# Attention and feed-forward on one core: projections dealt between the halves of second-layer units, a warmed beginning, and a last norm in halves

## The reference, cut to what matters

```python
qkv = (x @ w_qkv.T + b_qkv).reshape(b, n, 3, H, D).transpose(2, 0, 3, 1, 4)
q, k, v = qkv[0], qkv[1], qkv[2]
q, k = elu(q) + 1.0, elu(k) + 1.0
q, k = _apply_rope(q, sin, cos), _apply_rope(k, sin, cos)
attn = softmax(einsum('bhnd,bhmd->bhnm', q, k) * scale)
attn_out = einsum('bhnm,bhmd->bhnd', attn, v)
lepe = conv1d(v over the tokens, w_lepe, 3 taps, one channel each) + b_lepe
x = layernorm(x + attn_out + lepe)
# feed-forward: _conn_dense(k, h) is h @ where(k, 1, -1)
h = concatenate([x, -x]); h = relu(s0 * _conn_dense(k0, h)) * 2    # first layer, 1024 wide
h = relu(s1 * _conn_dense(k1, h)) * 2                              # second layer, 1024 wide
x = layernorm(x + s2 * _conn_dense(k2, h))                         # third layer, 256 wide
```

## Time and profile before

| | |
|---|---|
| median of 3 runs | 2167.17 us (2163.6 to 2169.74) |
| the profiled execution's own time | 2168.84 us |
| its span from first to last instruction | 2166.8 us |
| PE busy | 2077.0 us, 96% |
| DVE busy | 1696.8 us, 78% |
| ACT busy | 1499.5 us, 69% |
| POOL busy | 1008.6 us, 47% |
| first exponential of step 0 | 89.24 us |
| first and second batch, from first exponential to first exponential | 198.8 us, 238.5 us |
| each of the third to seventh | 254.7 us |
| last exponential | 2053.6 us |

### The profile page before, as it was taken

One profiled execution on the slowest core, in us unless ns is written; L12 is line 12 of the kernel. 1 busy time (PEld: TensorE's weight loads), 2 busy tenths in 40 slices (PEclk: granted clock), 3 DMA queues, 4 the chain that ended last, 5 costly groups with the idle time before them and its releaser, 6 DMA issues.

```text
span 2166.8 us, 43669 instructions
## 1 busy us (share of the span) xinstructions
PE 2077.0 (96%) x17136; PEld 836.7 (39%) x17136; DVE 1696.8 (78%) x3094; ACT 1499.5 (69%) x2867; POOL 1008.6 (47%) x578
## 2 busy tenths in 40 slices
PE   4899999999999999999999999999999999999988
PEld 2123333344433434334343443434343343434345
DVE  7978998787887887878787887878878788877143
ACT  3299888766777667776777767776677766767532
POOL 2849269432866157472584427761475704300000
PEclk8689999999999999999999999999999999999999
DMA  5101200010010200111001200002001110000000
GB/s 179 33 9 37 82 19 26 26 67 21 16 34 20 89 16 9 35 58 49 16 25 26 83 25 17 28 16 96 11 17 36 31 57 16 16 9 28 1 1 39
DMA packets 40428, 76.87 MB, mean 35 GB/s; under 512 B 15024, under 2 KB 19488, under 8 KB 37280
## 3 DMA queue, kind: packets, MB, share of 16 engines
q1 hardware_dynamic: 35040, 51.02, 8.2%
q0 software_dynamic: 5184, 23.07, 2.8%
HBM read 46.27 MB, written 25.17 MB: 33 GB/s over the span
## 4 chain that ended last, share of the span: by engine, by line
PE 79%; DVE 13%; ACT 5%; issue 2%; DMA 0%; POOL 0%; SPq 0%; POOLq 0%; ACTq 0%; DVEq 0%
PE unit_banks L723 25%; PE unit_banks L587 21%; PE o_bank L632 19%; DVE maxima L987 8%; PE unit_banks L736 5%; PE unit_banks L659 4%; ACT probs L814 3%; PE unit_banks L597 2%; PE unit_banks L647 1%; DVE hT L1056 1%; DVE h0T L1059 1%; DVE stats L1133 1%; PE unit_banks L640 0%; ACT work L856 0%; ACT work L855 0%
## 5 line engine op out<-in xcount | busy, mean ns | idle before, releaser
L987 DVE TENSOR_REDUCE maxima<-unit_banks 128x1 f32<-128x512 f32 x2048 | 1307.4, 684 | 326.2 <-PE unit_banks L587 321.3
L814 ACT ACTIVATE probs<-unit_banks 128x512 f32<-128x512 f32 x2048 | 1118.7, 599 | 540.3 <-PE unit_banks L597 536.5
L587 PE MATMUL unit_banks<-k_stack,q_stack 48*128 48x512 f16 x2048 | 660.3, 392 | 26.0 <-DVE maxima L987 22.4
L597 PE MATMUL unit_banks<-q_stack,k_stack 50*128 50x512 f16 x2048 | 657.3, 387 | 6.3 <-ACT probs L814 4.2
L632 PE MATMUL o_bank<-probs,v_pair 128*32 128x256 f32 x8192 | 565.4, 388 | 0.5
L723 PE MATMUL unit_banks<-h0T,w 128*128 128x512 f16 x2048 | 480.1, 380 | 0.0
L1385 POOL TENSOR_TENSOR attn<-o_rows_sb,rden 128x256 f32<-128x256 f32 x63 | 39.2, 622 | 787.9 <-DVE rden L1000 774.3
L587 PEld LDWEIGHTS unit_banks<-k_stack,q_stack 48*128 48x128 f16 x2048 | 155.1, 94 | 525.9 <-DVE maxima L987 273.5
L632 PEld LDWEIGHTS o_bank<-probs,v_pair 128*32 128x32 f32 x8192 | 207.5, 109 | 297.0 <-issue 216.9
L723 PEld LDWEIGHTS unit_banks<-h0T,w 128*128 128x128 f16 x2048 | 189.4, 98 | 222.8 <-issue 33.1
L597 PEld LDWEIGHTS unit_banks<-q_stack,k_stack 50*128 50x128 f16 x2048 | 155.5, 93 | 46.3 <-ACT probs L814 37.0
(11 more groups left out here) (148 smaller groups left out, 1664.0 us busy)
## 6 DMA issues: line engine op xcount, KB each, us to landing
rows<-in_x POOLq DMA_DIRECT2D x8, 1024.0 KB, 5.9
q_stack<-q_scratch SPq DMA_DIRECT2D x128, 64.0 KB, 2.0
k_stack<-k_scratch SPq DMA_DIRECT2D x128, 64.0 KB, 2.0
work<-in_xT SPq DMA_DIRECT2D x7, 1024.0 KB, 6.9
q_scratch<-parts POOLq DMA_DIRECT2D x14, 512.0 KB, 3.3
k_scratch<-parts POOLq DMA_DIRECT2D x14, 512.0 KB, 3.2
out<-rows SPq DMA_DIRECT2D x7, 1024.0 KB, 4.9
q_stack<-q_scratch SPq DMA_DIRECT2D x128, 32.0 KB, 1.9
```

Of the source, the lines that this page charges most:

```text
L587: nc.tensor.matmul(units.out(unit), q_stack[row:row + STACK, r, t * P:(t + 1) * P], k_stack[row:row + STACK, r, half * 512:(half + 1) * 51 ...
L597: nc.tensor.matmul(units.out(unit), k_stack[row:end, r, kt * P:(kt + 1) * P], q_stack[row:end, r, half * 512:(half + 1) * 512], start=True ...
L814: nc.scalar.activation(probs[:, 2 * (kt % 2) + h, half * 512:(half + 1) * 512], units.out(unit), ACT.Exp, scale=exp_regs[2 * (n % PAIRS) + ...
L987: nc.vector.reduce_max(maxima[:, v // T % 2, h * T + t, half:half + 1], units.out(unit), AXIS_X)\
```

## The change

1. **Table of the dense work.** `proj` units stand on every second step, from step 6 for Q (6, 8, 10, 12 instead of 6 to 9) and from step 28 for K (28, 30, 32, 34 instead of 32 to 35); in the second batch's projections, which run in the first batch, K has 22, 24, 26, 28 instead of 22 to 25. Pieces of `L1` units fill the steps between (7, 9, 11, 13 and 29, 31, 33, 35). The scale units move by one and three steps. The four input maxima stand on steps 55, 57, 59, 61 instead of 55 to 58, and the `bound` unit on step 62 instead of 59.
2. **Beginning.** 14 transposes of `ident` into `o_bank` on PE ahead of everything; POOL's load of the first rows (`load_x(0)`) moves behind its set-up and the arrival of the row constants; the nine small constants move on DVE ahead of the first elu, and the subtraction that makes `w0` is cut into two, one ahead of each `low_start`; all V results come after K's low part; K's scratch stores are issued by ACT; the Q stacks are loaded before K is stored.
3. **End.** POOL adds seven of the eight pairs of columns to the last rows as soon as they are there, DVE only the last one; the sums of that norm, its scales and the late units are interleaved in halves; the sums of the norm before it come after the first `L1` unit of the tail.

```diff
 Q_AT = 6
-K_AT, SCALE_AT = {1: 22}, ({}, {1: 28})
+K_AT, SCALE_AT = {1: 22}, ({}, {1: 31})
...
-INPUT_MAXIMA_AT, BOUND_AT = 55, 59
+INPUT_MAXIMA_AT, BOUND_AT = (55, 57, 59, 61), 62
 def k_at(c):
-    return K_AT.get(c, 32)
+    return K_AT.get(c, 28)
...
+WARM_UP = 14
...
-        deal(b + Q_AT, proj_units(c, 0))
+        for i, unit in enumerate(proj_units(c, 0)):
+            deal(b + Q_AT + 2 * i, [unit])
...
         if m < TAIL - 1:
-            deal(b + 26, hidden_units("L1", m, 0, range(3)))
+            deal(b + 26, hidden_units("L1", m, 0, range(1)))
+            for i, piece in enumerate(piece for u in hidden_units("L1", m, 0, range(1, 3)) for piece in pieces_of(u)):
+                at[b + 29 + 2 * i].append(piece)
...
-            deal(b + 74, hidden_units("L1", m, 1, range(6, KF)))
+            for i, piece in enumerate(piece for u in hidden_units("L1", m, 1, range(6, KF)) for piece in pieces_of(u)):
+                at[b + 71 + 2 * i].append(piece)
...
@@ SP, beginning
+            for i, half in enumerate((parts[:], parts_b)):
+                sp.wait_ge(start_split, i + 1)
+                sp.dma_start(q_scratch.ap()[0, :, i].rearrange("t p n -> p t n"), half).then_inc(start_written[i], 16)
+            for i in range(2):
+                sp.wait_ge(start_written[i], 16)
+            load_q_stack(0)
+            sp.dma_start(x_staged, xT[1]).then_inc(xT_loaded, 16)
+            load_q_stack(1)
             for i in range(2):
                 sp.wait_ge(start_written[i], 2 * 16)
...
@@ PE, beginning
+            pe.wait_ge(pool_setup, 4)
+            for _ in range(WARM_UP):
+                nc.tensor.transpose(o_bank[:, 0:P], ident[:], ident[:])
             pe.wait_ge(w_q_loaded, 16)
...
@@ ACT, beginning and tail
+            for i, half in enumerate((parts[:], parts_b)):
+                act.wait_ge(start_split, 3 + i)
+                act.dma_start(k_scratch.ap()[0, :, i].rearrange("t p n -> p t n"), half).then_inc(start_written[i], 16)
...
-                if unit[:3] == ("L1", TAIL, 0):
-                    normalise(NB - 2, 1, unit[3])
+                if unit[:3] == ("L1", TAIL, 0) and 3 <= unit[3] < 7:
+                    for t in range(2 * unit[3] - 6, 2 * unit[3] - 4):
+                        normalise(NB - 2, 1, t)
...
@@ DVE, beginning
+            def first_weights(kc):
+                if kc == 0:
+                    dve.wait_ge(k_loaded, 3 * 16)
+                then(nc.vector.tensor_tensor(w0[:, kc], k0_u8[:, kc], k0_u8[:, KC + kc], ALU.subtract))
...
             rotate(nc.vector.tensor_tensor, work[:], rotated)
             make_scale(("scale", 0, 0))
+            first_weights(0)
             low_start(0, work[:])
...
             rotate(nc.vector.tensor_tensor, work_of(0, 1), rotated)
-            v_out(("V", 0, 0))
-            v_out(("V", 0, 1))
             make_scale(("scale", 0, 1))
+            first_weights(1)
             low_start(1, work_of(0, 1))
-            v_out(("V", 0, 2))
-            v_out(("V", 0, 3))
+            for unit in v_units(0):
+                v_out(unit)
...
@@ DVE, end
-            for half in range(2):
-                span = slice(tiles(half).start, tiles(half).stop)
-                nc.vector.tensor_tensor(r[:, span, :], attn[:, span, :], r[:, span, :], ALU.add).then_inc(sum_ready, 1)
...
+            cols = slice(C - C // PAIRS, C)
+            nc.vector.tensor_tensor(r[:, :, cols], attn[:, :, cols], r[:, :, cols], ALU.add).then_inc(sum_ready, 1)
...
@@ POOL
-            load_x(0)
             nc.gpsimd.memset(v_pair[:], 0.0).then_inc(pool_setup, 1)
...
             pool.wait_ge(rows_loaded, 7 * 16)
+            load_x(0)
...
+            pool.wait_ge(attn_written, NB * PAIRS - 1)
+            seven = slice(0, C - C // PAIRS)
+            combine(rows_of(TAIL)[:, :, seven], attn[:, :, seven], rows_of(TAIL)[:, :, seven], ALU.add).then_inc(sum_ready, 1)
```

More of the change, by code:

```diff
@@ L59 @@
 SIDE_OPS = ELU_OPS + ROTATE_OPS + SPLIT_OPS
-START_OPS = (7, 8, 15, 16)
 SCALE_OPS = (2, 5)
@@ L90, in scale_at @@
 def scale_at(c, which):
-    return SCALE_AT[which].get(c, (14, 40)[which])
+    return SCALE_AT[which].get(c, (15, 40)[which])
 def pieces_of(unit):
@@ L493, in load_stacks, with load_k_stack @@
                     sp.dma_start(q_stack[row + lo_end:row + STACK, r], q_rows[b, hi, cols]).then_inc(stack_loaded[r], 16)
+            def load_k_stack(n):
+                b, j, r = n // PAIRS, n % PAIRS, n % RING
+                for h in range(2):
+                    cols = slice((2 * j + h) * N, (2 * j + h + 1) * N)
+                    hi, lo_end, row = slice(0, D), 2 * D, h * ROWS
                     sp.dma_start(k_stack[row:row + D, r], k_rows[b, hi, cols]).then_inc(stack_loaded[r], 16)
@@ L1204, in _, with rotated @@
                                                 ALU.mult, ALU.mult))
-            then(nc.vector.tensor_tensor(w0[:], k0_u8[:, 0:KC], k0_u8[:, KC:2 * KC], ALU.subtract))
+            for ct in range(2):
+                elu(0, ct)
+            join_sums(0, 0)
+            dve.wait_ge(rows_loaded, 7 * 16)
+            dve.wait_ge(elu_done, 2)
+            ops = [0]
+            def rotated(ins):
+                ops[0] += 1
+                ins.then_inc(start_rotated, 1)
+                if ops[0] in (2, 4):
+                    elu(0, 1 + ops[0] // 2)
+                if ops[0] == 4:
+                    join_sums(0, 1)
+                dve.wait_ge(start_rotated, ops[0])
+            rotate(nc.vector.tensor_tensor, work[:], rotated)
+            make_scale(("scale", 0, 0))
+            first_weights(0)
+            low_start(0, work[:])
+            dve.wait_ge(elu_done, 4)
+            rotate(nc.vector.tensor_tensor, work_of(0, 1), rotated)
+            make_scale(("scale", 0, 1))
+            first_weights(1)
+            low_start(1, work_of(0, 1))
+            for unit in v_units(0):
+                v_out(unit)
             then(nc.vector.tensor_scalar(w0[:], w0[:], s_work[:, 0:1], None, ALU.mult))
@@ L1491, in _ @@
                     split_x(b + 2)
-            ln_scales(NB - 1, 0)
+            pool.wait_ge(attn_written, NB * PAIRS - 1)
+            seven = slice(0, C - C // PAIRS)
+            combine(rows_of(TAIL)[:, :, seven], attn[:, :, seven], rows_of(TAIL)[:, :, seven], ALU.add).then_inc(sum_ready, 1)
+            for half in range(2):
+                ln_scales(TAIL, 0, half * T // 2, (half + 1) * T // 2)
             ln_scales(NB - 2, 1)
```

101 lines of the change are left out of this document (42 added, 59 removed).

## The result

| | before | after |
|---|---|---|
| median of 5 runs, us | 2168.97 (2163.6 to 2169.74) | 2188.72 (2187.92 to 2192.12) |
| ratio | | 1.0103, 95% interval 1.0091 to 1.0115 |
| profiled execution: own time, span | 2168.84, 2166.8 | 2192.12, 2189.9 |
| start to first exponential | 89.24 | 80.78 |
| first batch, second batch | 198.8, 238.5 | 206.9, 248.3 |

The kernel is slower by 1.0%. The direction was right and the size was not: 2178 was forecast. Beginning and end gave 8.5 and 7.6 us (forecast 7.3 and 7.4), the middle cost 39.2 (forecast 26.0). The error lies in the middle.

A forecast was written before the change was run, and what follows sets the result against it. PE was the engine to watch, busy 3.92 of a 3.92 us steady step. 2168.84 + 26.0 (middle) - 7.3 (beginning) - 7.4 (end) = 2180.1; the median lies 1.7 lower: 2178 us, range 2172 to 2184, with rivals 2158 to 2190.

The forecast's parts named there:

- bank waits, steps 36, 10, 62: Middle: PE waits for DVE to free banks, 1.82, 1.3 and 1.5 us a time, taken in full, +24.9 us.
- K spread, six batches: Middle, steps 28 to 36: spreading K's projections wins 0.8 us a batch, six times, -4.8 us.
- Q spread, third batch on: Middle, steps 6 to 14: spreading Q's projections taken as 0, from -1.5 to +1.5 us a batch.
- maxima and bound, second to sixth batch: Middle: input maxima and bound move between steps near 100%, taken as 0, between -2 and +2 us.
- second batch, Q and scale: Second batch: Q projections spread among empty steps cost 0.7 us each for four, from 30.21 to some 33, +2.8 us.
- first batch: First batch: spreading costs +2.7 us for K's run and about +0.8 for Q's, +3.5; bounds -2 and +7.
- beginning: Start: DVE's chain loses 4.0 us and starts 3.3 us earlier, -7.3 us, between -4 and -8.2.
- end: Tail: shorter waits and path -5.7 us, regained PE clock -1.7, together -7.4 us, between -2 and -8.5.
- absorbed: Rival, middle: PE's lost time comes back in steps held by ACT or DVE; 2153 us, faster, chance 0.13.
- cost half: Rival, middle: part of each bank wait is taken back; 2166 us, no change, chance 0.17.
- a rival, which had 2185 us: More clock dips in the first two batches cost 5 to 10 us; about 2185 us, slower, chance 0.12.
- the warm pace: Beginning: warm-up transposes bring the first products to full pace, worth 2.4 us of the earlier start.

The follow-up runs named there:

- exp. 2: Changed kernel, table untouched, but each unit on the three shared banks takes the one released first, not the next in turn: 2161.83 us, ratio 0.9968.
- exp. 6: New beginning and end, banks given by earliest release, old table except K projections of the second to seventh batch spread: 2143.85 us, ratio 0.9891.
- experiment 8: Changed kernel with freed banks, input maxima and bound back at their old steps, projections and scales still spread: 2155.50 us, ratio 0.9945.
- exp. 4: Changed kernel with the first batch's projections, scales, maxima and bound and the second's Q projections and scale at old steps: 2178.14 us, ratio 1.0047.
- experiments 1: Changed kernel with the old table of the middle, so only the new beginning and end remain: 2153.26 us, ratio 0.9921.
- experiment 7: Changed kernel, PE making the transposed scores twice in thin steps of the first two batches: 2188.70 us, ratio 1.0107.
- experiment 11: New ends, freed banks, K alone spread, plus transposed scores made twice in steps 9 to 13 and 15 to 17 of the first batch: 2142.63 us.
- 12: Changed kernel with freed banks, maxima and bound at old steps, plus transposed scores made twice in thin steps of the first two batches: 2154.22 us.
- experiment 3: Changed kernel, PE filling thin steps of the first two batches with eight transposes into the next unit's bank: 2191.65 us, ratio 1.0107.
- 9: Kernel with new ends, freed banks and K alone spread, without the 14 warm-up transposes: 2145.34 us, ratio 0.9895.
- 10: Kernel with new ends, freed banks and K alone spread, the 1 MB row load again first in GpSimd's queue: 2147.70 us, ratio 0.9906.

## Why the prediction was right in direction and wrong in size

By the prediction's own steps, with what the two traces and the experiments give (us, of the whole program):

| step of the prediction | forecast | measured | from |
|---|---|---|---|
| bank waits, steps 36, 10, 62 | +24.9 | +22.9 | 6 x 1.67, 5 x 1.33, 5 x 1.24 (exp. 2) |
| K spread, six batches | -4.8 | -5.2 | 6 x 0.87 (exp. 6) |
| Q spread, third batch on | 0 | +1.0 | what is left of the batches' +4.2 |
| maxima and bound, second to sixth batch | 0 | +3.3 | 5 x 0.65 (steps 59 to 62 in exp. 2 and 8) |
| second batch, Q and scale | +2.8 | +7.2 | 3.6 spreading, 3.6 clock (exp. 4, 8) |
| first batch | +3.5 | +8.1 | Q 3.7, K 1.5, steps 58 to 63 2.2, step 2 0.7 |
| a clock fall in the sixth batch | 0 | +1.65 | 7.19 against 5.54 in step 36 |
| last batch | -0.4 | +0.3 | the traces |
| middle | +26.0 | +39.3 (39.2 by the spans) | |
| beginning | -7.3 | -8.5 | first exponential |
| end | -7.4 | -7.6 | tail |

**Banks: right.** Each wait had the place and nearly the price that was read from the earlier trace rows: 1.67 for 1.82, 1.33 for 1.3, 1.24 for 1.5. The rivals in which they are absorbed or cost half fell with experiment 2. The sentence that PE takes its products in order and the lead is not in the banks carried the whole direction.

**The failed step is the clock in the middle.** The forecast left it at nothing ("Bounds -2 and +7: the clock dips there and may dip elsewhere") and gave it to a rival, which had 2185 us and a chance of 0.12 and came nearest; the price that it named, 5 to 10 us, holds. In the changed kernel half clock stood for 13.7 us in steps 9 to 15 of the first batch, 3.4 in its step 62, 10.2 in steps 12 to 15 of the second batch and 3.4 in step 36 of the sixth; before, for 13.7 us in steps 11, 12, 17 and 18 of the first batch and nowhere else in the middle (the trace's record of the granted clock, without the stretch around the first exponential). The Trainium skill's sentence on the throttled default ("TensorE: Matmul & The Clock Gate", What's actually happening) spoke for this, and the trace agrees in the second batch: 10.2 us at the lower level against none. In the first batch's thinned steps it shows no more of it than before. My account of the excess of 13: 3.6 in the second batch (experiment 8 has these steps at full clock); in the first 2.0 (1.3 in step 62 by experiment 2, and 0.7 in step 2); 1.65 in the sixth. That is 7.3. I priced a spread projection by what ACT and PE have to do in the step, at full pace. But a thin step with a fall is PE's at half pace: step 15 of the second batch has 4.77 us of PE's work in 4.77. The profiled run had more of it than most (own time 2192.1, mean clock 0.979; three of the five runs took 2187.9 to 2188.7 at 0.980 to 0.982), so the error against the median is 10.7, not 12.

**The second failed step is maxima and bound at nothing.** The forecast took one full step for another, and gave it bounds of -2 and +2. With the banks freed, step 62 is still 0.60 longer than before and step 61 0.28, and step 59 is 0.23 shorter. Steps 61 and 62 of the fourth batch in experiment 2 (L1110 is the last input maximum, L1114 joins the maxima, L1016 takes row maxima, L609 is a score product, L714 is the bound's product):

```profile
1028.35 0.66 DVE L1110 TENSOR_REDUCE in_max<-work 128x1 f32<-128x512 f32 x1
...
1029.05 0.16 DVE L1114 TENSOR_REDUCE in_bound<-in_max 128x1 f32<-128x4 f32 x1
1029.12 0.74 DVE L1162 BATCH_NORM_STATS2 stats<-rows 128x6 f32<-128x256 f32 x2
...
1029.78 2.47 DVE L1016 TENSOR_REDUCE maxima<-unit_banks 128x1 f32<-128x512 f32 x4
...
1030.52 0.39 PE L609 MATMUL unit_banks<-k_stack,q_stack 48*128 48x512 f16 x1 [0.21 <-DVE maxima L1016]
...
1031.11 0.39 PE L609 MATMUL unit_banks<-k_stack,q_stack 48*128 48x512 f16 x1 [0.21 <-DVE maxima L1016]
...
1031.43 0.38 PE L714 MATMUL unit_banks<-ln_consts,in_bound 128*128 128x1 f32 x2
```

In step 61 DVE now has the last input maximum beside the split of the row maxima's bank and the norm's sums; the row maxima come late, and PE waits for them twice before its next scores. The bound's product does not wait itself; it takes its 0.25 us before PE's dense piece in step 62 instead of in step 59. With the first batch's 0.9 this part makes 4.2 of the 13.

**The rest.** Spreading over thin steps cost 3.6 in the second batch, not 2.8. In the first batch Q cost 3.7, not 0.8, and K 1.5, not 2.7. That Q's 3.7 is the spreading and not more of the low clock is seen in steps 9 to 18: the kernel before and the changed one, both with 13.7 us at half clock there, and then experiments 1 and 2 (old and new table), both with 10.2:

```profile
117.90:154.44 36.54, 34.21 (x257) 9.81 (x254) 25.67 (x48) 32.65 (x62) 10.84 (x5) 0.81 0.05 13
110.09:150.36 40.27, 36.73 (x265) 11.80 (x265) 26.23 (x48) 33.57 (x65) 10.83 (x5) 0.83 0.05 11
112.60:147.80 35.20, 32.88 (x261) 9.65 (x262) 26.24 (x48) 32.15 (x61) 10.84 (x5) 0.85 0.05 13
109.44:148.30 38.86, 35.22 (x265) 11.15 (x265) 26.22 (x48) 33.55 (x64) 10.84 (x5) 0.87 0.05 12
```

The new table is 3.7 us longer in both pairs. Q's part of the steady batches lost 0.2 each instead of nothing. With the banks' -2.0, K's -0.4 and the last batch's 0.7 these add 1.8.

**Beginning: right within its bounds but for 0.3,** since the earlier start was 4.4 us (bound 4.1) and DVE's chain 4.1 shorter (forecast 4.0). Of the start, the load's removal gives more than the warm pace, 2.85 against 1.54 in the rows. The forecast had 2.5 and 2.4 and allowed only 3.3 for both; they were had in full, 4.4. Part of the first may not be a matter of the DMA engines: with the load first, DVE's own setup also started 1.34 us later (5.11 against 3.77), since GpSimd made its constants later. The Trainium skill's rule ("Trainium Kernel Development and Optimization", Key Constraints) that all queues share the 16 engines agrees with the input's landing 2.63 us later, where 2.5 was worked out from the row.

**What stays open.** That falls follow thin work or a pause of PE is read from where they stand. That feeding PE removes them is shown in the first batch: the three kernels with doubled products (7, 11, 12) have none in steps 6 to 18, and the other eleven all have. In the second batch it is not: the fed kernels 3, 7 and 12 had none in steps 6 to 15, but neither had 8, in which nothing was fed. The falls vary from one execution to the next, and each kernel has one trace. The time never came back in full: falls stood in other thin or waiting places. Whether the feeding moved them there is not shown, since unfed kernels fell in the same places (steps 27 and 28 of the first batch in 2, 4, 8 and 9, step 17 of the second in 8, step 7 of the last in 4 and 10). A single fall's 1.3 to 1.7 us is certain only where the same step was seen with and without it. I did not find the version of the spread table in which no fall is left.

## What to carry to other kernels

Before units are woven into each other, list for each bank who used it last and when that user's last reader comes; a bank given out in turn made waits of 1.1 to 1.6 us here that one given out by earliest release did not (26.9 us in all, for five lines). Spreading work paid only where K's projections went among full steps (0.87 us a batch); Q's among full steps lost 0.2, and among thin steps 3.6 to 3.7. When the profile shows clock falls in a stretch that a change makes thinner, put their price into the sum and not only into a rival.

The best version here is the old table with K alone spread, freed banks and the new ends: 2143.9 us, 1.1% faster than before (with doubled products, experiment 11, it can't be told from that).

## What was not expected of the hardware

A wait of PE of 1.6 us in an otherwise full stretch can be enough to be followed by a fall: in the four kernels with this wait (the changed one, 3, 4 and 7) step 36 took 5.54 us in most batches and 7.1 to 7.2 in four of 24, with half clock from about the first product behind the wait, and experiment 3 has one behind the wait of step 62; in the eight kernels with freed banks no step 36 had a fall. And feeding PE did not end the falls: in experiment 7 the first batch was at full clock from 88.6 to 177.4 us, and half clock came at 177.39, 416.32, 935.15 and 1853.34.
